# A gated cross-attention and ternary FFN block: hidden activations transposed by DMA instead of TensorE, and a second PSUM bank for down

## The reference

```python
def _quant_weight(w):
    scale = jnp.mean(jnp.abs(w)) + EPS
    return jnp.clip(jnp.round(w / scale), -1.0, 1.0), scale
def _quant_act(x):
    s = jnp.max(jnp.abs(x), axis=-1, keepdims=True) / 127.0 + EPS
    return jnp.clip(jnp.round(x / s), -128.0, 127.0), s
def _qlinear(x, w):
    wq, ws = _quant_weight(w)
    xq, xs = _quant_act(x)
    return jnp.einsum('bsi,oi->bso', xq, wq) * xs * ws
...
# attention: softmax(where(mask, -inf, (ctx Wq + bq)(ctx Wk + bk) * H**-0.5 * layernorm(x)))
x = x + jnp.tanh(g_xattn[0]) * attention(ctx, layernorm(x))
h = layernorm(x)
hidden = silu(_qlinear(h, w_gate)) * _qlinear(h, w_up)       # 2048 wide
x = x + jnp.tanh(g_ffn[0]) * _qlinear(hidden, w_down)
```

## Time and profile before

| | |
|---|---|
| median of 3 runs | 255.97 us (255.76 to 256.09) |
| the profiled execution's own time | 255.76 us |
| its span | 254.0 us |
| TensorE (PE) busy | 221.0 us, 87% |
| VectorE (DVE) busy | 194.4 us, 77% |
| ScalarE (ACT) busy | 165.8 us, 65% |
| GpSimd (POOL) busy | 138.1 us, 54% |

### The profile page before, as it was taken

How to read it: one execution, slowest core, us unless ns; L and a number is a source line. 1 busy time by engine, 2 the same in 40 slices (tenths; PEclk the granted TensorE clock), 3 DMA queues, 4 the chain that set the end, 5 groups by cost and what they waited for, 6 DMA issues and landing times.

```text
span 254.0 us, 3485 instructions
## 1 busy us (share of the span) xinstructions
PE 221.0 (87%) x1174; PEld 110.3 (43%) x1174; DVE 194.4 (77%) x356; ACT 165.8 (65%) x202; POOL 138.1 (54%) x191
## 2 busy tenths in 40 slices
PE   8700455989969899999999999999999999999994
PEld 6200152434424355544544544544544554445551
DVE  0699988897999789898988766879677851949621
ACT  2776958996985964447977437494963483754760
POOL 3975999998976998714297930310978400000000
PEclk9975555799999999999999999999999999999999
DMA  7999819960000010100011110000111101000112
GB/s 261 419 417 430 312 50 406 385 235 2 0 0 3 0 43 12 62 12 0 3 41 41 43 44 0 0 4 0 43 41 44 43 0 44 0 0 0 44 41 83
DMA packets 7041, 22.89 MB, mean 90 GB/s; under 512 B 624, under 2 KB 752, under 8 KB 5488
## 3 DMA queue, kind: packets, MB, share of 16 engines
q1 hardware_dynamic: 6880, 22.55, 22.8%
q10 hardware_dynamic: 144, 0.13, 0.2%
HBM read 18.48 MB, written 4.19 MB: 89 GB/s over the span
## 4 chain that ended last, share of the span: by engine, by line
PE 67%; POOL 15%; DVE 9%; issue 6%; DMA 2%; ACT 1%; SPq 0%; DVEq 0%; POOLq 0%
PE pD L900 22%; PE pU L870 18%; PE pG L857 17%; PE pT L888 5%; POOL stage_a L412 3%; POOL stage_b L412 3%; PE pA L835 3%; DMA hid<-in_masks 2%; POOL mask_bias L346 1%; DVE hid L1295 1%; POOL probs L381 1%; PE pA L845 1%; DVE st L1202 1%; DVE hid L1300 1%; POOL sd L371 1%
## 5 line engine op out<-in xcount | busy, mean ns | idle before, releaser
L619 ACT ACTIVATE hid<-pG,act_g 128x512 f32<-128x512 f32 x64 | 43.6, 687 | 37.8 <-PE pG L857 37.5
L857 PE MATMUL pG<-gate_w,xqT 128*128 128x512 bf16 x256 | 65.1, 387 | 1.8 <-ACT hid L619 1.1
L870 PE MATMUL pU<-up_w,xqT 128*128 128x512 bf16 x256 | 63.3, 379 | 3.7 <-DVE hid L1295 2.7
L900 PE MATMUL pD<-down_w,hidT 128*128 128x512 bf16 x256 | 58.7, 379 | 0.4 <-DVE stage_b L1323 0.4
L1295 DVE TENSOR_TENSOR hid<-pU,hid 128x512 f32<-128x512 f32 x64 | 43.6, 685 | 14.2 <-PE pU L870 11.6
L632 ACT ACTIVATE hidT<-pT 128x1024 bf16<-128x1024 f16 x32 | 32.2, 1020 | 20.6 <-PE pD L900 10.4
L870 PEld LDWEIGHTS pU<-up_w,xqT 128*128 128x128 bf16 x256 | 24.4, 98 | 36.0 <-DVE hid L1295 5.0
L419 POOL TENSOR_SCALAR out_scale<-den,act_u,down_k 128x1 f32<-128x1 f32 x16 | 6.4, 404 | 60.4 <-DVE den L1310 60.4
L857 PEld LDWEIGHTS pG<-gate_w,xqT 128*128 128x128 bf16 x256 | 24.7, 99 | 33.1 <-issue 6.0
L900 PEld LDWEIGHTS pD<-down_w,hidT 128*128 128x128 bf16 x256 | 24.5, 98 | 29.5 <-DVE stage_b L1323 0.7
L625 ACT ACTIVATE hid<-hid,magic_c,inv 128x1024 f32<-128x1024 f32 x24 | 29.4, 1237 | 4.1 <-DVE inv L1313 4.1
(11 more groups left out here) (103 smaller groups left out, 306.9 us busy)
## 6 DMA issues: line engine op xcount, KB each, us to landing
stage_a<-in_L_ffn_w_gate SPq DMA_DIRECT2D x4, 1024.0 KB, 10.4
stage_b<-in_L_ffn_w_up SPq DMA_DIRECT2D x4, 1024.0 KB, 18.8
stage_a<-in_L_ffn_w_down SPq DMA_DIRECT2D x4, 1024.0 KB, 5.8
stage_b<-in_x SPq DMA_DIRECT2D x2, 1024.0 KB, 5.8
out<-x SPq DMA_DIRECT2D x8, 256.0 KB, 2.0
out<-stage_b SPq DMA_DIRECT2D x8, 256.0 KB, 2.0
ctx_s<-in_ctx SPq DMA_DIRECT2D x4, 256.0 KB, 6.9
x<-in_x SPq DMA_DIRECT2D x2, 512.0 KB, 7.3
```

The costliest lines, as they stand in the source:

```text
L619: act.activation(hid[:, t % NH, n * 512:(n + 1) * 512], pG[n % 2][:, :], ACT.Silu, scale=act_g[:, t:t + 1]).then_inc(silu_done, 1)
L857: ins = pe.matmul(pG[n % 2][:, :], xqT[:, t // TILES % 2, t % TILES, k, :], gate_w[:, n, k, :], start=k == 0, stop=k == KD - 1)
L870: ins = pe.matmul(pU[n % 2][:, :], xqT[:, t // TILES % 2, t % TILES, k, :], up_w[:, n, k, :], start=k == 0, stop=k == KD - 1)
L900: ins = pe.matmul(pD[:, :], hidT[:, k, :], down_w[:, k // KD, k % KD, :], start=k == 0, stop=k == KI - 1)
```

## The change

- The quantised hidden half stays in float32, rounded by adding 1.5 x 2^23; all 32 halves are quantised on ScalarE. GpSimd subtracts the constant again and writes bf16 (`hidden_16`). SP then transposes 128x1024 values from SBUF to SBUF with a DMA transpose. TensorE's `transpose_hidden` and ScalarE's `copy_hiddenT` are gone. The bf16 values and hidT have two buffers each (tile t and t + 2 share one), in chunks 2 and 3 of stage_b, where the up weights were staged.
- The two banks of pT become a third bank of pU and a second one of pD.
- VectorE's five ternary chunks no longer come rounded from GpSimd: it multiplies by the inverse scale, takes the minimum with 1, and writes 16-bit integers, then the maximum with -1 into bf16. GpSimd rounds 7 chunks instead of 12.
- Small operations on 2 or 4 columns with two tensors become one operation per column with a scalar operand: `exp_bias`, `gate_sums`, `inverse_x`, `inverse_hidden`.
- All engines' orders are written anew, with SP's transposes among its stores.

```diff
-        hidT = sb("hidT", [P, KI, P], BF16)
+NG, NU, ND = 2, 3, 2
+        hid16 = stage_b[:, 2, :].bitcast(BF16).rearrange("p (r i) -> p r i", r=2)
+        hidT = stage_b[:, 3, :].bitcast(BF16).rearrange("p (r k t) -> p r k t", r=2, t=P)
...
-        ROUND_BY = ["PPPP", "PPPP", "PPPP"]
+        ROUND_BY = ["-P-P", "-P-P", "P-PP"]
...
+        def short_free(engine, t, h):
+            if t >= 2:
+                engine.wait_ge(hidT_ready[t % 2][h], 16 * (t // 2))
+            else:
+                wait_ternary(engine, 1, 2)
...
+            def transpose_hidden(t, h):
+                wait_short(sp, t, h)
+                if t >= 2:
+                    sp.wait_ge(down_half, 2 * (t - 2) + h + 1)
+                else:
+                    wait_ternary(sp, 1, 3)
+                sp.dma_start_transpose(hidT[:, t % 2, 8 * h:8 * h + 8, :], hid16[:, t % 2, h * 1024:(h + 1) * 1024])\
+                  .then_inc(hidT_ready[t % 2][h], 16)
...
+            def hidden_16(t, h):
+                short_free(pool, t, h)
+                wait_quantised(pool, t, h)
+                out16, part = short_args(t, h)
+                pool.tensor_scalar(out16, part, -ROUND, 1.0, ALU.add, ALU.mult).then_inc(h16_pool, 1)
...
                     if t >= NH:
-                        act.wait_ge(hidT_done, 2 * (t - NH) + 2)
+                        wait_short(act, t - NH, 0)
+                        wait_short(act, t - NH, 1)
...
-                if c >= 2:
-                    pe.wait_ge(prod_done, c - 1)
+                if c >= NU:
+                    pe.wait_ge(prod_done, c - NU + 1)
...
-                elif quarter == 0:
-                    pe.wait_ge(final_ready, t)
+                if quarter == 0:
+                    if t < ND:
+                        pe.wait_ge(scored, TILES)
+                    else:
+                        pe.wait_ge(final_ready, t - ND + 1)
                 if quarter % 2 == 0:
-                    pe.wait_ge(hidT_ready, 2 * t + quarter // 2 + 1)
+                    pe.wait_ge(hidT_ready[t % 2][quarter // 2], 16 * (t // 2 + 1))
...
-                dve.scalar_tensor_tensor(negb[:, t0:t1], mx[:, t0:t1], -1.0, rstd1[:, t0:t1], ALU.mult, ALU.mult)\
-                   .then_inc(negb_ready, 1)
+                for t in range(t0, t1):
+                    dve.tensor_scalar(negb[:, t:t + 1], mx[:, t:t + 1], rstd1[:, t:t + 1], -1.0, ALU.mult, ALU.mult)\
+                       .then_inc(negb_ready, 1)
...
-                dve.tensor_scalar(chunk, stages[m][:, n, :], ROUND, 1.0, ALU.subtract, ALU.min).then_inc(w_upper, 1)
+                dve.tensor_scalar(chunk.bitcast(I16), stages[m][:, n, :], winv[:, m:m + 1], 1.0, ALU.mult, ALU.min)\
+                   .then_inc(w_upper, 1)
                 dve.wait_ge(w_upper, count(SIGN_BY, "V", m, n))
-                dve.tensor_scalar(chunk, chunk, -1.0, None, ALU.max).then_inc(w_ready_dve, 1)
+                dve.tensor_scalar(chunk, chunk.bitcast(I16), -1.0, None, ALU.max).then_inc(w_ready_dve, 1)
```

More of the change, by code:

```diff
@@ L979, in _ @@
             down(1, 0)
+            pe.wait_ge(q_ready, 4)
+            transpose_x(2)
             down(1, 1)
+            gate(4, 0)
+            pe.wait_ge(xqT_ready, 3)
+            score(8)
+            gate(4, 1)
+            gate(4, 2)
+            pe.wait_ge(scored, 9)
+            score(9)
+            gate(4, 3)
+            gate(5, 0)
             down(1, 2)
             down(1, 3)
-            pe.wait_ge(k_ready, 4)
-            transpose_x(2)
-            up(3, 2)
-            up(3, 3)
@@ L1137, in _ @@
             gate(12, 3)
-            transpose_hidden(11, 0)
-            transpose_hidden(11, 1)
+            up(12, 3)
             gate(13, 0)
+            up(13, 0)
+            down(10, 3)
             gate(13, 1)
+            up(13, 1)
+            pe.wait_ge(xqT_ready, 7)
+            transpose_x(7)
+            gate(13, 2)
+            up(13, 2)
+            gate(13, 3)
+            up(13, 3)
+            gate(14, 0)
+            up(14, 0)
+            gate(14, 1)
+            up(14, 1)
+            gate(14, 2)
+            up(14, 2)
+            gate(14, 3)
+            up(14, 3)
+            gate(15, 0)
+            up(15, 0)
+            gate(15, 1)
+            up(15, 1)
+            gate(15, 2)
+            up(15, 2)
+            gate(15, 3)
+            up(15, 3)
             down(11, 0)
@@ L1406, in _ @@
-            reciprocal_scale(0)
-            score(5)
-            weight_ternary(1, 2)
-            copy_xT(1)
-            mask_and_max(5)
+            mask_and_max(4)
+            stats1(6)
+            score(5)
+            stats1(7)
+            mask_and_max(5)
+            copy_xT(1)
+            reciprocal_scale(1)
+            weight_scale(2)
+            product(0, 0)
+            score(6)
+            weight_ternary(2, 1)
+            mask_and_max(6)
+            score(7)
             product(0, 1)
-            reciprocal_scale(1)
+            mask_and_max(7)
@@ L1441, in _ @@
[L1441 removed]
             product(2, 3)
[L1443 removed]
+            stats1(8)
             absmax_hidden(2, 1)
[L1445 to L1453 removed]
+            product(3, 0)
+            absmax_x(5)
+            inverse_hidden(2)
+            inverse_x(2)
+            stats1(9)
@@ L1454, in _ @@
+            product(3, 1)
+            stats2(6)
+            product(3, 2)
+            residual2(0)
+            product(3, 3)
+            reciprocal_scale(2)
             copy_xT(2)
             absmax_x(6)
-            product(3, 2)
+            stats1(10)
+            stats2(7)
+            score(8)
+            absmax_hidden(3, 0)
             absmax_x(7)
-            product(3, 3)
+            score(9)
             inverse_x(3)
+            mask_and_max(8)
             absmax_hidden(3, 1)
```

926 lines of the change are left out of this document (439 added, 487 removed).

## The result

The changed kernel takes 242.72 us (median of 4, 242.31 to 243.02), the kernel before 255.87 on the same chip: a ratio of 0.948, 95% interval 0.947 to 0.950. Forecast were 241.0 us. The profiled execution took 242.59 us with a span of 240.8.

The account below looks back on a forecast made before the run. Others pace the kernel up to 77 us, then only TensorE's list counts. Start 68.5 + list 160.8 + gaps 6.2 + tail 0.5 + end 3.2 = 239.2 us span, plus 1.8: 241.0; range 235 to 246, chance 0.51.

Parts of the forecast that it names:

- TensorE's list: TensorE's work behind up(2,1): 183 groups at 0.864 plus 2.7, 160.8 us; 13.4 us of hidden transposes gone.
- The start: Up to up(2,1), paced by VectorE: up(2,1) at 68.5 us, 5.9 us gained.
- Taking 0.15 ... product(2,0) comes at ... 71.5: VectorE's start: one-column operations at 0.15 us and other list changes bring product(2,0) from 78.2 to 71.5 us.
- I take its present 1.21 us: VectorE's first ternary pass, now also multiplying and writing integers, stays at 1.21 us; upper bound 2.28.
- The small operations: VectorE's start: five operations of 6.57 us become 12 one-column ones of 1.8, 4.8 less; others 0.2 more.
- The gaps: TensorE's idle time behind up(2,1): 4 us from VectorE's lack of room beside 2.2 of before, 6.2 us.
- tail: The five last downs, down(11) to down(15), held by DMA transposes in SP's queue: 0.5 us at 2.4 each.
- Nothing else in its work changes: On TensorE, beyond the lost half transposes: the same groups in another order.
- The DMA transposes: SP's queue: 2.4 us per half tile in series, 2.0 plus 0.4 for issue.
- the formula: Last half down ends at 219.9 + 6d + 1.73, d being us per half transpose; covered up to d = 2.3.
- the rival that was written: GpSimd becomes the bound, three batches of 16-bit passes each waiting 3 us more: 250 us; chance 0.12.
- The third rival: The start gives nothing: one-column operations wait or ternary passes take up to 2.28 us; 247, both 252; chance 0.12.

Follow-up runs that it names:

- small_rounds: The changed kernel with GpSimd rounding only the first 64 of 2048 columns in each of its 7 chunks; 232.60 us.
- copy_first: The changed kernel with copy_xT(0) moved ahead of weight_ternary(1, 0) and stats2(2) on VectorE; 240.97 us.
- stt_back: The changed kernel with the small VectorE operations back as two-tensor operations on 2 or 4 columns (one per tile for den2); 243.61 us.
- two_up_banks: The changed kernel, but from up(3, 0) on an up group waits as if pU had two banks, not three; 245.81 us.
- one_down_bank: The changed kernel with one bank for down instead of two; 253.48 us.
- dma_twice: The changed kernel with a second DMA transpose of the same size, into a spare buffer, ahead of each of the 32; 255.57 us.

## Why the prediction came out near, point by point

The time came out 1.7 us above the forecast partly by luck: up(2,1) came 6.6 us late, and 4.5 us of gaps that were forecast didn't come.

- **TensorE's list: right.** 13.4 us were taken for the transposes, and doubling them costs 13.1. TensorE's busy time, 204.7, is in the 203 to 207 that was named.
- **The start: mis-sized.** The step that was off is "Taking 0.15 ... product(2,0) comes at ... 71.5", and within it the ternary pass "I take its present 1.21 us". product(2,0) started at 77.67, 6.2 later. The view that gave 1.21 had two more forms of the same pass:

```profile
L1357 DVE TENSOR_SCALAR up_w<-stage_b 128x2048 bf16<-128x2048 f32 x2 | 3.0, 1494 | 0.0
L1357 DVE TENSOR_SCALAR down_w<-stage_a 128x2048 bf16<-128x2048 f32 x1 | 1.6, 1640 | 0.0
```

  The two long ones of before, 1.78 us at 53.21 and 1.64 at 69.24, end 1.1 us behind the end of a GpSimd pass, as the one of 41.03 in the changed kernel does. Ten passes took 11.65 us before (7.06 and 4.59), which the base of 78.2 holds; now they take 15.5: 10.4 for the first (1.80, 1.27, 3.00, 1.40, 2.90) and 5.1 for the second. That is 3.8 us more. VectorE's idle time up to product(2,0) rose from 9.8 to 11.0 us (74.20 less 64.44 busy, 73.64 less 62.66), where 0.7 less was forecast: 1.9 us, and the wait of 1.76 for the scale of up_w is nearly as much. The remaining 0.5 is the sum of smaller differences, a residual of 2.37 us among them. With GpSimd's roundings short the passes are 1.28 to 1.34 (small_rounds), so the operation was costed rightly and its neighbour was not. The trace of before had one more sign: GpSimd's centring at 33.03 us took 2.16 us, 0.69 elsewhere, beside a residual and a ternary pass of VectorE. copy_xT(0) behind a ternary chunk was put at "about 1 us" for gate(0,0), which came 4.4 later than before (46.43 against 42.05); copy_first gives 3.6 of that back, 1.8 in time.
- **The small operations: right as a sum of rows, wrong as a property of the form.** Ahead of product(2,0) they fell from 7.7 to 3.4 us, 4.3 less where 4.8 less 0.2 was forecast. But with the old form back (stt_back) they take 4.7 us there: some 3 of the 4.3 went with the old order, whose overlaps with GpSimd they were. The form itself is worth about 0.9 us of time, not clear of noise.
- **The gaps: mis-sized the other way.** "That is no room at all, and every wait in it becomes a TensorE gap": 1.7 us in all instead of 6.2, with VectorE busier than forecast (57.90 of 63.00). The third up bank, counted for the start only, took 3.1 us of waits (two_up_banks), some two thirds of the error. This and the start nearly cancel: +6.6 (start), -4.5 (gaps) and -0.5 (tail) make +1.6 of span.
- **The second bank of down: left out.** "Nothing else in its work changes" costed it at nothing without its cover. It is worth 10.8 us in this order (one_down_bank). The change as a whole wasn't hurt by the omission, as the sum had no wait there, but with one bank only 2.4 us would be left of the gain. The removal of the transposes and the bank are one edit: the first takes away what hid the residual, the second replaces it.
- **The DMA transposes: the price nearly twice too high, the formula too kind.** They were taken at 2.4 us each in series; they come every 1.37 us, so the tail cost nothing. The slack was put too wide: "covered up to d = 2.3 us", other runs of downs "up to about 2.9", "at d = 3.8 ... no gain left". Doubled, at some 2.7 us per half, the tail lost 5.2 us where the formula gives 2.6, the other downs 2.4 where it gives nothing, and the gain was gone. In the tail it left out the two stores in the same queue, 1.4 us, and that a transpose lands 3.0 us after its issue (3.2 in dma_twice), of which some 1.9 come behind the last issue. The two estimates that the prediction took from the Trainium skill don't hold for this form of transpose: 0.7 us per half, by the full DMA speed (Advanced Engine Details and Errata, X-Bar Transpose (TRN2)), is half of the 1.37 measured, and 10.5, by eight times the time of one block (VectorE: DVE Perf Modes, The three transpose paths), is over seven times it.
- **GpSimd: right in its passes.** The 16-bit passes took 1.05 us (1.12 taken); 54.25 of 63.00 us in the second stretch (52.8 forecast). TensorE waited for it only through the first transpose, 1.37 us. As a source of overlap in the start it was the cause, which isn't the rival that was written.
- **The third rival** ("the start gives nothing", 247 or 252 us) was right in its passes of over 2 us and nearly in the start (2.0 us gained), and wrong in the time, since the gaps it kept beside them weren't there.

## What to carry to other kernels

Where a change frees one engine's passes from waiting for another's, ask what now runs at the same time: an overlap can cost more than the wait did. Here it showed in the trace as one form whose longest row was up to three times its shortest; price such a form by its shortest row and by what will run beside it, not by its mean or by one group of it. Take a bank's or buffer's price from what stands next to it in the new order, since work that is removed may have been a cover. For a queue's slack, count the series spacing and the landing of the last transfer apart.

## What the runs showed of the hardware

- A DMA transpose of 128x1024 16-bit values from SBUF to SBUF holds SP's queue for 1.23 us, follows the one before after 1.37 us and lands after 3.0 us; a plain store of 256 KB on the same queue is issued in 0.33 to 0.35 us at the median. 32 of these transposes take the count of packets under 512 B from 624 to 34416.
- VectorE's f32 to int16 pass over 2048 values takes 1.27 us alone and up to 3.00 beside GpSimd's rounding; int16 to bf16 0.69 and up to 2.35; a residual of 512 values 0.74 and up to 2.37. Operations on one column with a scalar operand were never longer than 0.22 us; with two tensors, two columns took 1.01 us (L1266) and 0.51 (L1314) on the mean in stt_back.
